# Grouped attention in a decoder kernel: causal zeros written by GpSimd behind the exponential, the second pass without mask matmuls, the last values in the next step

## The chip, the cores and the metric

One core of one Trainium2 chip runs the whole program. The metric is device microseconds of one execution. The engines are PE (TensorE), DVE (VectorE), ACT (ScalarE), GpSimd (POOL in the rows) and SyncE (SP), which only issues DMAs here. The five run in parallel, each in its own order, and wait for one another by semaphores.

## The reference

Two decoder layers of six sublayers on x of [4, 512, 128], float32. The change lies in one sublayer, grouped attention (B = 4, S = 512, 16 heads of 8, 4 groups of 4 heads that share keys and values):

```python
xr = rope(x)
Q = (xr @ Wq).reshape(B, S, N_HEADS, D_K).transpose(0, 2, 1, 3)
Q = Q.reshape(B, N_GROUPS, HPG, S, D_K)
K = (xr @ Wk).reshape(B, S, N_GROUPS, D_K).transpose(0, 2, 1, 3)
V = (xr @ Wv).reshape(B, S, N_GROUPS, D_K).transpose(0, 2, 1, 3)
scores = jnp.einsum('bghsd,bgtd->bghst', Q, K) / jnp.sqrt(jnp.float32(D_K))
mask = jnp.triu(jnp.full((S, S), -1000000000.0, dtype=scores.dtype), k=1)
attn = jax.nn.softmax(scores + mask, axis=-1)
out = jnp.einsum('bghst,bgtd->bghsd', attn, V)
```

The mask is causal: a query sees the keys up to its own place.

## The kernel before

The program runs stage after stage. In `grouped_attention` a first part makes the rotated queries and keys, split into three bf16 parts, and lays them down in DRAM; then the block `ga2` does the attention in 16 steps, `it = GROUPS * b + g`, one for each batch b and group g. Each step works on 512 x 512 scores of four heads, in chunks of 128 (`CH` = 4). It has two passes over the scores:

- First pass, `max_scores(b, g, n)`, n = 0 to 15, c = n // 4 the chunk of queries and i = n % 4 the head: queries on the partitions, keys up to the diagonal on the columns, in `psA[:, n % 2]`. The diagonal block gets the mask by a matmul of `ident_bf` with `mask_bf`, onto which the scores are accumulated. DVE's `maxima` takes the maximum of each row out of it (L1831). Score n waits for maximum n-2, since `psA` has two halves. Below, "score n" and "maximum n" are these.
- The maxima are turned on PE (`turn_maxima`), split into three bf16 parts on DVE (`split_maxima`, five instructions, L1840 to L1844), and sent by SyncE as three further rows of `q` (`put_maxima`, L1660), so that the second pass subtracts them inside the matmul.
- Second pass, `attend(b, g, n)`, n = 0 to 7, c = n // 2 the chunk of keys and n % 2 the pair of heads: keys on the partitions, queries from the diagonal on, two heads, in `psB[:, n % 2]`. ACT takes the exponential of it into `att` (L1810). attend(n) waits for exponential n-2.
- `values(b, g, c)`: four matmuls in float32 (L1754), one a head, accumulate `va` times `att` over c into `psO`; the last increments `o_mm`. ACT copies `psO` (`copy_out`), PE turns the copy (`turn_out`, L1768), and DVE divides by the sums and stores (`output`, L1851 and L1852, two instructions).

The order on each engine is written out by hand in the `step` functions. The first pass runs two steps ahead of the second: the step of `it` has score 2n and 2n+1 of `it + 2` ahead of each attend(n) of `it`, and the turning and the split of `it + 1`. Steps are unrolled for the first and last batch and loop with `Fori` between. SyncE loads `q` and `k` for the next batch when `o_mm` says that the step is done (`q_load`, L1578 and L1580), and behind that the maxima of the next step. GpSimd copies each step's values into `va` and does nothing else. In the first four steps ACT also issues loads of the next stage's weights (`preload`).

Of the kernel before, what the change touches and what calls it, by code (L numbers as in the profile page):

```python
# [20 lines left out]
ALU = mybir.AluOpType  # L21
# [3 lines left out]
P = 128  # L25
BATCH, SEQ, D = 4, 512, 128
TOKENS = BATCH * SEQ
TILES = TOKENS // P
CH = SEQ // P
# [1424 lines left out]
def grouped_attention(nc, A, x, xn, xnT, ident, preload=None):  # L1454
# [12 lines left out]
    with Stage(nc, "ga") as st:  # L1467
# [130 lines left out]
        with Stage(nc, "ga2") as s2:  # L1598
# [18 lines left out]
            m_rows = [s2.sem(f"m_rows{n}") for n in range(2)]  # L1617
            b_scores = s2.sem("b_scores")
            b_exp = s2.sem("b_exp")
            o_mm = s2.sem("o_mm")  # L1620
            o_copied = s2.sem("o_copied")
            o_turned = s2.sem("o_turned")
# [30 lines left out]
            with s2.block() as block:  # L1653
# [26 lines left out]
                @block.gpsimd  # L1680
                def _(pool):
                    pool.memset(va[:, :, :, :], 0.0).then_inc(va_clean, 1)
                    pool.wait_ge(va_clean, 1)
                    pool.memset(va[:, :, :, DH:DH + 1], 1.0).then_inc(va_clean, 1)
                    pool.wait_ge(va_clean, 2)

                    def step(b, g):

                        pool.wait_ge(o_mm, GROUPS * b + g - 1)
                        pool.tensor_copy(va[:, g % 2, :, 0:DH], v[:, bass.ds(CH * b, CH), DH * g:DH * g + DH]).then_inc(va_ready, 1)  # L1690

                    for g in range(GROUPS):
                        if g >= 2:
                            pool.wait_ge(o_mm, g - 1)
                        pool.tensor_copy(va[:, g % 2, :, 0:DH], v[:, 0:CH, DH * g:DH * g + DH]).then_inc(va_ready, 1)
                    with pool.Fori(1, BATCH) as b:
                        for g in range(GROUPS):
                            step(b, g)

                @block.tensor  # L1700
                def _(pe):
# [25 lines left out]
                    def attend(b, g, n):  # L1727

                        it = GROUPS * b + g
                        if n == 0:  # L1730
                            pe.wait_ge(m_rows[g % 2], 96 * b + 48 * (g // 2) + 48)
                        c, pair = n // 2, n % 2
                        if not (first(it, 1) and n < 2):

                            pe.wait_ge(b_exp, 8 * it + n - 1)
                        for i in range(2):
                            keys, queries = k[0:SPLIT + MROWS, g, P * c:P * c + P], q[0:SPLIT + MROWS, g, 2 * pair + i, :]
                            if c < CH - 1:
                                pe.matmul(psB[:, n % 2, i, P * c + P:SEQ], keys, queries[:, P * c + P:SEQ], start=True, stop=True)
                            out = psB[:, n % 2, i, P * c:P * c + P]  # L1740
                            pe.matmul(out, ident_bf[:, :], mask_bf[:, 1, :], start=True, stop=False)
                            mm = pe.matmul(out, keys, queries[:, P * c:P * c + P], start=False, stop=True)  # L1742
                        mm.then_inc(b_scores, 1)

                    def values(b, g, c):

                        it = GROUPS * b + g
                        if c == 0:
                            pe.wait_ge(va_ready, it + 1)
                            if not first(it, 1):  # L1750
                                pe.wait_ge(o_copied, it)
                        pe.wait_ge(b_exp, 8 * it + 2 * c + 2)
                        for i in range(HPG):
                            mm = pe.matmul(psO[VW * i:VW * i + VW, P * c:SEQ], va[:, g % 2, c, :], att[:, g % 2, c, i, P * c:SEQ],  # L1754
                                           start=(c == 0), stop=(c == CH - 1), skip_group_check=True)
                        if c == CH - 1:
                            mm.then_inc(o_mm, 1)
# [13 lines left out]
                    def step(b, g):  # L1771
                        it = GROUPS * b + g
                        for n in range(CH * HPG // 2):
                            if exists(it + 2):
                                for m in (2 * n, 2 * n + 1):
                                    max_scores(*ahead(b, g, 2), m)
                            attend(b, g, n)
                            if n == 1 and exists(it + 1):
                                turn_maxima(*ahead(b, g, 1))
                            if n == 4 and not first(it, 1):  # L1780
                                turn_out(*ahead(b, g, -1))
                            if n % 2 == 1 and n >= 3:
                                values(b, g, (n - 3) // 2)
                        values(b, g, CH - 1)

                    for n in range(CH * HPG):
                        max_scores(0, 0, n)
# [1 line left out]
                    for n in range(CH * HPG):  # L1789
                        max_scores(0, 1, n)  # L1790
                    schedule(pe, step)
                    turn_out(BATCH - 1, GROUPS - 1)

                @block.scalar
                def _(act):
                    def copy_out(it):
                        act.wait_ge(o_mm, it + 1)
                        if not first(it, 1):
                            act.wait_ge(o_turned, it)
                        act.activation(oT[:, :], psO[:, :], ACT.Copy).then_inc(o_copied, 1)  # L1800

                    def step(b, g):
                        it = GROUPS * b + g
                        for n in range(CH * HPG // 2):
                            c, pair = n // 2, n % 2
                            act.wait_ge(b_scores, 8 * it + n + 1)
                            if n == 0 and not first(it, 2):

                                act.wait_ge(o_mm, it - 1)
                            act.activation(att[:, g % 2, c, 2 * pair:2 * pair + 2, P * c:SEQ], psB[:, n % 2, :, P * c:SEQ], ACT.Exp,  # L1810
                                           scale=SCALE).then_inc(b_exp, 1)
                            if n == 1 and not first(it, 1):
                                copy_out(it - 1)
                        if first(it, GROUPS) and preload is not None:
                            preload(act, g, GROUPS)

                    schedule(act, step)
                    copy_out(STEPS - 1)

                @block.vector  # L1820
                def _(dve):
# [35 lines left out]
                    def step(b, g):  # L1857
                        it = GROUPS * b + g
                        for n in range(CH * HPG):
                            if exists(it + 2):  # L1860
                                maxima(*ahead(b, g, 2), n)
                            if n == 5 and exists(it + 1):
                                split_maxima(*ahead(b, g, 1))
                            if n == 9 and not first(it, 1):
                                output(*ahead(b, g, -1))

                    for n in range(CH * HPG):
# [790 lines left out]
```

## Time and profile before

| | us |
|---|---|
| median of 3 runs (1525.8 to 2162.62) | 1527.76 |
| the profiled execution | 1530.27 |
| its span | 1528.5 |
| one steady step of the attention, 393.89 to 404.84 | 10.95 |
| the 16 steps, first exponential to last values, 325.01 to 496.84 | 171.8 |

Busy shares of the span: PE 71%, DVE 62%, ACT 49%, GpSimd 33%. These are averages over stages with different limits; the stage of the change takes some 11% of the span. The span is the profiled execution from its first to its last instruction; its own time is 1.8 us more, and it stands 2.5 us above the median.

### The profile page before, as it was taken

The page shows a single profiled execution, that of the slowest core. Times are in us where ns is not written, and L with a number is a line of the kernel's source. Part 1 is how long each engine was busy: PE and PEld are TensorE (multiplying, and loading weights), DVE is VectorE, ACT ScalarE, POOL GpSimd, SP SyncE. Part 2 cuts the span into 40 slices and gives each one's busy share as a digit, 9 for nine tenths or more (in the row PEclk, how much of TensorE's full clock was granted, in tenths as well). Part 3 has the DMA queues.
Part 4 walks back from the last instruction along what each step waited for, and adds up shares of the span by engine and source line. Part 5 has one row for each costly group of instructions (what it writes and reads, how often), then busy time and mean ns, then how long its engine had stood idle before and what let it go on. Part 6 is the DMA issues. An engine that isn't in the chain of part 4 may idle for free. (4 is left out here: it accounts for less than half of the span.)

```text
span 1528.5 us, 17644 instructions
## 1 busy us (share of the span) xinstructions
PE 1077.8 (71%) x5325; PEld 478.6 (31%) x5326; DVE 945.6 (62%) x1906; ACT 748.7 (49%) x779; POOL 497.3 (33%) x402
## 2 busy tenths in 40 slices
PE   5886932589999549999460658988778877345584
PEld 2533321256665415555230001112112111035353
DVE  6625688367785542222353799999999998265201
ACT  3102622225556302323132159999999999821232
POOL 0000000200000024554110177787886876100463
PEclk9897965669999659999775555555655556565698
DMA  4000000124110101101214100100100000031012
GB/s 157 0 0 25 0 0 17 64 70 164 38 34 12 37 11 28 29 29 28 66 36 142 49 25 21 39 23 24 39 21 28 34 21 1 0 113 32 21 39 75
DMA packets 55665, 60.78 MB, mean 40 GB/s; under 512 B 11130, under 2 KB 43460, under 8 KB 55599
## 3 DMA queue, kind: packets, MB, share of 16 engines
q1 hardware_dynamic: 45294, 45.54, 9.4%
q0 software_dynamic: 3968, 8.13, 2.1%
q10 hardware_dynamic: 6336, 6.29, 1.3%
q8 instruction: 34, 0.56, 0.2%
q14 instruction: 33, 0.26, 0.1%
HBM read 44.35 MB, written 15.34 MB: 39 GB/s over the span
## 5 line engine op out<-in xcount | busy, mean ns | idle before, releaser
L2339 POOL TENSOR_TENSOR hb_t<-hb_t,hb_r 128x1024 f32<-128x1024 f32 x124 | 330.1, 2702 | 199.0 <-ACT hb_r L2285 199.0
L2351 DVE TENSOR_SCALAR hb_dpos<-hb_psR 128x1024 f32<-128x1024 f32 x128 | 155.7, 1217 | 23.4 <-PE hb_psR L2214 18.7
L2223 PE MATMUL hb_psR<-ha_q,ha_k 20*128 20x512 bf16 x256 | 123.0, 578 | 59.8 <-DVE hb_dpos L2351 59.6
L2214 PE MATMUL hb_psR<-ha_q,ha_k 78*128 78x512 bf16 x256 | 123.4, 583 | 48.2 <-DMA ha_k<-hsx 39.7
L2359 DVE SCALAR_TENSOR_TENSOR hb_t<-hb_psR,hb_dpos 128x1024 f32<-128x1024 f32 x128 | 155.1, 1212 | 0.0
L2235 PE MATMUL hb_psO<-hb_t,ha_va 128*9 128x512 f32 x512 | 112.3, 977 | 51.8 <-ACT hb_t L2308 51.8
L1831 DVE TENSOR_REDUCE ga_nm<-ga_psA 128x1 f32<-128x128 f32 (+3 forms) x256 | 112.9, 484 | 47.5 <-PE ga_psA L1717 47.4
L1810 ACT ACTIVATE ga_att<-ga_psB 128x1024 f32<-128x1024 f32 (+3 forms) x128 | 87.0, 709 | 99.9 <-PE ga_psB L1742 99.9
L2368 DVE SCALAR_TENSOR_TENSOR hb_r<-hb_t 128x1024 f32<-128x1024 f32 x64 | 127.3, 1990 | 0.0
L2308 ACT ACTIVATE hb_t<-hb_t 128x4096 f32<-128x4096 f32 x32 | 113.8, 3603 | 0.0
L1315 DVE TENSOR_TENSOR m2x_e_h<-m2x_e_act_out,m2x_e_psG 128x512 f32<-128x512 f32 x39 | 26.8, 688 | 130.6 <-ACT m2x_e_act_out L1284 93.7
L1585 POOL MEMSET ga_q<- 64x8192 bf16 x1 | 6.9, 6920 | 276.4 <-POOLq L1512 276.4
L2285 ACT ACTIVATE hb_r<-hb_r 128x4096 f32<-128x4096 f32 x16 | 57.9, 3619 | 71.1 <-DVE hb_r L2368 70.9
L1284 ACT ACTIVATE m2x_e_act_out<-m2x_e_psU 128x512 f32<-128x512 f32 x39 | 23.3, 598 | 124.8 <-PE m2x_e_psG L1227 124.8
L2214 PEld LDWEIGHTS hb_psR<-ha_q,ha_k 78*128 78x128 bf16 x256 | 19.6, 113 | 168.4 <-DVE hb_t L2359 64.7
L1716 PE MATMUL ga_psA<-ga_mask_bf,ga_ident_bf 128*128 128x128 bf16 x256 | 56.7, 235 | 17.8 <-PEq L250 15.7
L206 PE MATMUL ln_tp<-all_ident,all_xn 128*128 128x128 f32 x80 | 23.9, 455 | 63.0 <-DVE all_xn L165 62.2
L191 ACT ACT_TABLE_LOAD x6 | 7.7, 1283 | 122.5 <-PEq L118 118.5
L2223 PEld LDWEIGHTS hb_psR<-ha_q,ha_k 20*128 20x128 bf16 x256 | 15.8, 103 | 162.6 <-DVE hb_dpos L2351 144.7
L1714 PE MATMUL ga_psA<-ga_k,ga_q 72*128 72x128 bf16 (+2 forms) x192 | 55.1, 298 | 8.4 <-DVE ga_nm L1831 6.3
L2303 ACT ACTIVATE hb_t<-hb_t,ha_one 128x4096 f32<-128x4096 f32 x16 | 59.4, 3711 | 0.2
L2292 ACT ACTIVATE hb_t<-hb_t,ha_one 128x4096 f32<-128x4096 f32 x16 | 59.1, 3694 | 0.0
(448 smaller groups left out, 2289.9 us busy)
## 6 DMA issues: line engine op xcount, KB each, us to landing
ga_q<-qx SPq DMA_DIRECT2D x48, 96.0 KB
ha_q<-hqx SPq DMA_DIRECT2D x48, 96.0 KB
ha_k<-hkx SPq DMA_DIRECT2D x16, 288.0 KB
hsx<-ha_aparts SPq DMA_DIRECT2D x6, 384.0 KB
hy_fwd<-in_const_fwd_dram SPq DMA_DIRECT2D x1, 2048.0 KB, 8.1
hy_inv<-in_const_inv_dram SPq DMA_DIRECT2D x1, 2048.0 KB
f_up<-in_L_ffn_W_dram ACTq DMA_DIRECT2D x4, 512.0 KB, 3.9
f_gate<-in_L_ffn_W_dram ACTq DMA_DIRECT2D x4, 512.0 KB, 5.6
```

The source lines that it names most:

```text
L1810: act.activation(att[:, g % 2, c, 2 * pair:2 * pair + 2, P * c:SEQ], psB[:, n % 2, :, P * c:SEQ], ACT.Exp, scale=SCALE).then_inc(b_exp, 1)
L1831: dve.tensor_reduce(nm[:, g % 2, i, c:c + 1], psA[:, n % 2, 0:P * c + P], AX.X, ALU.max, negate=True).then_inc(a_max, 1)
L2214: mm = pe.matmul(psR[:, dist_slot(n), i, :], k[0:ROWS, it % 2, i0 + i, P * c:P * c + P], q[0:ROWS, it % 2, i0 + i, :], start=True, stop=True)
L2223: mm = pe.matmul(psR[:, side_slot(n), i, :], k[SIDE:SIDE + SROWS, it % 2, i0 + i, P * c:P * c + P], q[SIDE:SIDE + SROWS, it % 2, i0 + i, : ...
L2235: mm = pe.matmul(psO[32 * i:32 * i + VW, :], va[:, CH * (it // G) + c, HPG * (it % G) + i, :], t[:, (2 * it + c % 2) % T_QUADS, 2 * (c // ...
L2292: act.activation(quad(t, it, 1), quad(t, it, 1), ACT.Sqrt, bias=one[:, 0:1]).then_inc(root_ready, 1)
L2303: act.activation(tt, tt, ACT.Ln, scale=2.0, bias=one[:, 0:1]).then_inc(ln_ready, 1)
L2308: act.activation(tt, tt, ACT.Exp, scale=(-1.0, -2.0)[form]).then_inc(w_ready, 1)
L2339: pool.tensor_tensor(tt, tt, r[:, (2 * it + form) % R_QUADS, k, :], ALU.add).then_inc(sum_ready, 1)
L2351: dve.tensor_scalar(dpos[:, n % 2, :], psR[:, dist_slot(n), :, :].rearrange("p i t -> p (i t)"), 0.0, None, ALU.max).then_inc(dpos_ready, 1)
L2359: dve.scalar_tensor_tensor(out=unit(t, n), in0=psR[:, side_slot(n), :, :].rearrange("p i t -> p (i t)"), scalar=CAP, in1=dpos[:, n % 2, :] ...
L2368: dve.scalar_tensor_tensor(out=unit(r, n), in0=tt, scalar=1.0, in1=tt, op0=ALU.add, op1=ALU.mult).then_inc(m_ready, 1)
```

## The change

- GpSimd gets a new function `causal`: behind every second exponential it overwrites the diagonal blocks of chunk c (four heads of 128 x 128) in `att`, in place, with `affine_select`, which keeps what lies on the causal side and puts 0.0 elsewhere. It increments a new semaphore `masked`, for which `values` waits in place of `b_exp`. GpSimd's steps are unrolled for all 16.
- `attend` has no mask matmul: one matmul a head from the diagonal to the end, in place of up to three (16 matmuls of mask fewer in a step, and the diagonal block joined to the rest). The first pass keeps its masks.
- On PE values(0) moves from behind attend(3) to behind attend(4), values(1) from behind attend(5) to behind attend(6), values(2) and values(3) from the end of the step into the next one, behind attend(0) and attend(1). `turn_out` moves from behind attend(4) to behind attend(5).
- On ACT `copy_out` moves from behind exponential 1 to behind exponential 2; on DVE `output` moves from behind maximum 9 to behind maximum 12.

```diff
+                    def causal(b, g):
+                        it = GROUPS * b + g
+                        for c in range(CH):
+                            pool.wait_ge(b_exp, 8 * it + 2 * c + 2)
+                            block_c = att[:, g % 2, c, :, P * c:P * c + P]
+                            pool.affine_select(block_c, block_c, [[0, HPG], [1, P]], ALU.is_ge, 0.0, base=0, channel_multiplier=-1).then_inc(masked, 1)
...
+                    for b in range(BATCH):
                         for g in range(GROUPS):
-                            step(b, g)
+                            if GROUPS * b + g >= 2:
+                                pool.wait_ge(o_mm, GROUPS * b + g - 1)
+                            pool.tensor_copy(va[:, g % 2, :, 0:DH], v[:, CH * b:CH * b + CH, DH * g:DH * g + DH]).then_inc(va_ready, 1)
+                            causal(b, g)
...
-                            if c < CH - 1:
-                                pe.matmul(psB[:, n % 2, i, P * c + P:SEQ], keys, queries[:, P * c + P:SEQ], start=True, stop=True)
-                            out = psB[:, n % 2, i, P * c:P * c + P]
-                            pe.matmul(out, ident_bf[:, :], mask_bf[:, 1, :], start=True, stop=False)
-                            mm = pe.matmul(out, keys, queries[:, P * c:P * c + P], start=False, stop=True)
+                            mm = pe.matmul(psB[:, n % 2, i, P * c:SEQ], keys, queries[:, P * c:SEQ], start=True, stop=True)
...
-                        pe.wait_ge(b_exp, 8 * it + 2 * c + 2)
+                        pe.wait_ge(masked, CH * it + c + 1)
...
-                            if n == 4 and not first(it, 1):
+                            if n < 2 and not first(it, 1):
+                                values(*ahead(b, g, -1), 2 + n)
+                            if n in (4, 6):
+                                values(b, g, (n - 4) // 2)
+                            if n == 5 and not first(it, 1):
                                 turn_out(*ahead(b, g, -1))
-                            if n % 2 == 1 and n >= 3:
-                                values(b, g, (n - 3) // 2)
-                        values(b, g, CH - 1)
...
-                            if n == 1 and not first(it, 1):
+                            if n == 2 and not first(it, 1):
                                 copy_out(it - 1)
...
-                            if n == 9 and not first(it, 1):
+                            if n == 12 and not first(it, 1):
                                 output(*ahead(b, g, -1))
```

On PE, before, from attend(3) (L1739 to L1742) over values(0) to score 8 of a steady step (L1714 to L1717):

```order
L1739 MATMUL ga_psB<-ga_q,ga_k 128x256
L1741 MATMUL ga_psB<-ga_mask_bf,ga_ident_bf 128x128
L1742 MATMUL ga_psB<-ga_q,ga_k 128x128
L1754 MATMUL ga_psO<-ga_att,ga_va 32x512 [waits ga2_b_exp,ga2_o_copied,xa_ln1_stats_ready]
L1754 MATMUL ga_psO<-ga_att,ga_va 32x512 x3
L1714 MATMUL ga_psA<-ga_k,ga_q 128x256 [waits ln1_copied]
```

The same place now, from attend(3) (L1741) over scores 8 and 9 (L1717 to L1720) and attend(4) to values(0) (L1753):

```order
L1741 MATMUL ga_psB<-ga_q,ga_k 128x384
L1717 MATMUL ga_psA<-ga_k,ga_q 128x256 [waits ln1_copied]
L1719 MATMUL ga_psA<-ga_mask_bf,ga_ident_bf 128x128
L1720 MATMUL ga_psA<-ga_k,ga_q 128x128
L1717 MATMUL ga_psA<-ga_k,ga_q 128x256 [waits ln1_copied]
L1719 MATMUL ga_psA<-ga_mask_bf,ga_ident_bf 128x128
L1720 MATMUL ga_psA<-ga_k,ga_q 128x128
L1741 MATMUL ga_psB<-ga_q,ga_k 128x256 [waits ga2_b_exp]
L1741 MATMUL ga_psB<-ga_q,ga_k 128x256
L1753 MATMUL ga_psO<-ga_att,ga_va 32x512 [waits ga2_masked,ga2_o_copied,xa_ln1_stats_ready]
```

Between attend(3) and score 8, which waits for DVE (its semaphore is printed as `ln1_copied`, an old name of the same number), there is no longer a block of values.

On DVE, around the output (L1851, L1852) before:

```order
L1844 TENSOR_TENSOR ga_nmp<-ga_nmr,ga_nmp 16x128
L1831 TENSOR_REDUCE ga_nm<-ga_psA 128x1 x4
L1851 RECIPROCAL ga_rs<-ga_psT 128x16
L1852 TENSOR_TENSOR ga_oa<-ga_psT,ga_rs 128x4x32
L1831 TENSOR_REDUCE ga_nm<-ga_psA 128x1 x12
```

and now (L1853, L1854):

```order
L1846 TENSOR_TENSOR ga_nmp<-ga_nmr,ga_nmp 16x128
L1833 TENSOR_REDUCE ga_nm<-ga_psA 128x1 x7
L1853 RECIPROCAL ga_rs<-ga_psT 128x16
L1854 TENSOR_TENSOR ga_oa<-ga_psT,ga_rs 128x4x32
L1833 TENSOR_REDUCE ga_nm<-ga_psA 128x1 x9
```

Four maxima stood between the split and the output, and seven stand there now: the output is between the first and the second of the four widest.

## Rows read from the trace of the kernel before

**Rows 1.** Windows; columns: stretch, length, busy us of each engine, PEclk, DMA share, GB/s.
```profile
393.89:404.84 10.95, 10.53 (x129) 6.87 (x127) 8.60 (x23) 5.80 (x9) 0.21 (x1) 1.00 0.12 38
481.86:489.71 7.85, 7.11 (x83) 3.97 (x82) 1.82 (x7) 5.69 (x10) 0.00 (x0) 1.00 0.02 4
489.71:497.00 7.29, 6.29 (x74) 3.33 (x72) 0.55 (x2) 5.77 (x10) 0.00 (x0) 1.00 0.00 0
498.00:500.00 2.00, 1.05 (x9) 0.86 (x7) 0.55 (x2) 0.00 (x0) 0.00 (x0) 0.87 0.00 0
```

**Rows 2.** Table of waits, 320 to 500 us: total, times, longest.
```profile
PEld ga_psA L1714 <- DVE ga_nm L1831: 33.4, 69, 0.8
```

**Rows 3.** Timeline of PE in a steady step: start, us, engine, line, operation.
```profile
393.01 0.22 PE L1716 MATMUL ga_psA<-ga_mask_bf,ga_ident_bf 128*128 128x128 bf16 x1
...
393.29 0.22 PE L1741 MATMUL ga_psB<-ga_mask_bf,ga_ident_bf 128*128 128x128 bf16 x1
393.35 0.22 PE L1742 MATMUL ga_psB<-ga_q,ga_k 75*128 75x128 bf16 x1
...
394.60 0.22 PE L1714 MATMUL ga_psA<-ga_k,ga_q 72*128 72x128 bf16 x1
...
396.51 1.06 PE L1754 MATMUL ga_psO<-ga_att,ga_va 128*32 128x512 f32 x8
397.51 0.28 PE L1714 MATMUL ga_psA<-ga_k,ga_q 72*128 72x256 bf16 x1
...
397.76 0.28 PE L1714 MATMUL ga_psA<-ga_k,ga_q 72*128 72x256 bf16 x1
...
399.70 0.85 PE L1754 MATMUL ga_psO<-ga_att,ga_va 128*32 128x384 f32 x8
400.49 0.34 PE L1714 MATMUL ga_psA<-ga_k,ga_q 72*128 72x384 bf16 x1
...
403.97 0.22 PE L1716 MATMUL ga_psA<-ga_mask_bf,ga_ident_bf 128*128 128x128 bf16 x1
```

**Rows 4.** Timeline of PE at the end of the last step but one.
```profile
488.00 1.01 PE L1754 MATMUL ga_psO<-ga_att,ga_va 128*32 128x256 f32 x16
488.94 0.34 PE L1739 MATMUL ga_psB<-ga_q,ga_k 75*128 75x384 bf16 x1
```

**Rows 5.** Timeline of DVE in the same steady step.
```profile
394.97 0.76 DVE L1831 TENSOR_REDUCE ga_nm<-ga_psA 128x1 f32<-128x256 f32 x2 [0.47 <-PE ga_psA L1717]
395.64 0.27 DVE L1840 COPY ga_nmT<-ga_psT 16x128 f32<-16x128 f32 x1
...
396.19 0.28 DVE L1842 TENSOR_TENSOR ga_nmr<-ga_nmT,ga_nmp 16x128 f32<-16x128 f32 x1
...
398.98 0.26 DVE L1851 RECIPROCAL ga_rs<-ga_psT 128x16 f32<-128x16 f32 x1
...
399.59 1.01 DVE L1831 TENSOR_REDUCE ga_nm<-ga_psA 128x1 f32<-128x384 f32 x2
400.98 2.53 DVE L1831 TENSOR_REDUCE ga_nm<-ga_psA 128x1 f32<-128x512 f32 x4 [0.37 <-PE ga_psA L1717]
```

**Rows 6.** GpSimd's groups by line, with mean ns.
```profile
L2339 POOL TENSOR_TENSOR hb_t<-hb_t,hb_r 128x1024 f32<-128x1024 f32 x124 | 330.1, 2702 | 199.0 <-ACT hb_r L2285 199.0
...
L1586 POOL MEMSET ga_k<- 64x2048 bf16 x1 | 1.8, 1798 | 0.0
```

**Rows 7.** Timeline of ACT, the last exponential of the step.
```profile
403.04 0.39 ACT L1810 ACTIVATE ga_att<-ga_psB 128x256 f32<-128x256 f32 x1 [1.17 <-PE ga_psB L1742]
```

**Rows 8.** Line 2368, DVE, a later stage: min/median/max ns.
```profile
L2368 DVE SCALAR_TENSOR_TENSOR hb_r<-hb_t x64: 1206/1916/3441, 854.9 to 1289.2; 128x1024 f32<-128x1024 f32 x64
```

**Rows 9.** Timeline of SyncE's queue in the same step: loads, then maxima.
```profile
393.16 2.64 SPq L1578 DMA_DIRECT2D ga_q<-qx  x3
...
397.06 1.84 SPq L1660 DMA_DIRECT2D ga_q<-ga_nmp  x3
```

**Rows 10.** Line 1660, the maxima's DMAs, 345 to 382 us: issue to landing.
```profile
DMA to landing us min/median/max: 2.2/2.3/5.6
```

More of the change, by code:

```diff
@@ L1619, in grouped_attention @@
             b_exp = s2.sem("b_exp")
+            masked = s2.sem("masked")
             o_mm = s2.sem("o_mm")
@@ L1685, in _ @@
                     pool.wait_ge(va_clean, 2)
[L1687 to L1696, printed above, removed]
+                    def causal(b, g):
[5 more added lines that the diff above has]
+                    for b in range(BATCH):
                         for g in range(GROUPS):
-                            step(b, g)
+                            if GROUPS * b + g >= 2:
+                                pool.wait_ge(o_mm, GROUPS * b + g - 1)
+                            pool.tensor_copy(va[:, g % 2, :, 0:DH], v[:, CH * b:CH * b + CH, DH * g:DH * g + DH]).then_inc(va_ready, 1)
+                            causal(b, g)
                 @block.tensor
@@ L1791, in _ @@
                     schedule(pe, step)
+                    values(BATCH - 1, GROUPS - 1, 2)
+                    values(BATCH - 1, GROUPS - 1, 3)
                     turn_out(BATCH - 1, GROUPS - 1)
```

## Prediction

> **What bounds the kernel now.** First the windows by stage: a step of the grouped attention (one batch, one group; 16 in all) takes 10.95 us at the granted clock 1.00, with PE recorded busy for 10.53 us and DVE for 8.60, ACT for 5.80, GpSimd for 0.21 [rows 1]. That reads like PE alone, but the table of waits says otherwise: PE's weight loads for the first pass's scores waited 33.4 us for DVE's maxima, 69 times [rows 2]. The two engines hold each other: psA has two halves, so score n can't start before maximum n-2 is done. The reader should therefore not ask how busy PE is but which waits close the loop around a step. Followed in the timelines, from score 1 of one step to score 1 of the next, it falls into six stretches [rows 3, 5]:
> (a) PE, score 1 to score 4: 393.01 to 394.60, 1.59 us. (b) Score 4 until DVE takes it: 0.37. (c) DVE, maximum 4 (394.97), maximum 5, the split of the maxima (from 395.64), maxima 6 and 7, which let score 9 start at 397.76: 2.79. (d) PE, score 9 to score 12 (400.49): 2.73. (e) Score 12 until DVE takes it (400.98): 0.49. (f) From there to the next score 1 (403.97): 2.99; DVE runs four maxima of 512 columns in it without a pause (2.53), PE ends it with values(2) and values(3). The sum is 10.96.
> values(0), 396.51 to 397.51 [rows 3], lies inside (c): PE does it while DVE splits. values(2) and values(3) lie inside (f), while DVE does its last maxima.
>
> **The change, part by part.**
> Mask matmuls of the second pass: each occupies 0.06 us of PE (393.29 to 393.35) [rows 3], and joining the diagonal block to the rest costs nothing more, since the columns are the same. Per step 16 go: 0.96 us of PE's issue. That is the gain to be had: 15 us in 16 steps if PE alone set the pace.
> Values: values(0) moves from behind attend(3) to behind attend(4), values(1) from attend(5) to attend(6), values(2) and (3) into the next step behind attend(0) and attend(1). Now the same six stretches:
> (a) loses four mask matmuls (0.24) and takes in values(2) and values(3). Where they are not kept waiting they take 0.94 (488.00 to 488.94) [rows 4]; as two blocks each has a gap of its own ahead of it, which I put at 0.09 (the values' weights are loaded anew, and wait for a semaphore), so 1.12. 1.59 - 0.24 + 1.12 = 2.47, or +0.88.
> (b) stays 0.37.
> (c) stays 2.79: it is DVE's own work. But values(0) is no longer in it, so PE is through with attend(3) at what was 396.3 and stands at score 8 until maximum 6 is done at what was 397.4: about 1.1 us.
> (d) takes values(0), 1.00, in place of values(1), 399.70 to 400.49 or 0.79 [rows 3], and loses 0.24 of masks: 2.70, or -0.03.
> (e) stays 0.49.
> (f) DVE's output moves from behind maximum 9 to behind maximum 12, so its 0.61 us (398.98 to 399.59) [rows 5] falls into the unbroken run: 2.53 + 0.61 + 0.05 for the signal (about what the maximum's end leaves before PE moves) = 3.19, or +0.20. PE's own way through (f) is shorter, since values(2) and (3) are gone from it.
> New loop: 2.47 + 0.37 + 2.79 + 2.70 + 0.49 + 3.19 = 12.01 us, against 10.96: **+1.05 a step**. The masks go where PE waits anyway; the values leave the two places where they were free. Twelve steps have the whole loop: +12.6.
> The ends: step 0 has no values of a step before it and only saves, at most 0.96; I take -0.7. The thirteenth loop lacks the next step's first scores: +0.3. The last two steps have no first pass; ACT and PE share them (5.69 and 7.11 busy of 7.85) [rows 1], the masks save up to 0.96 in the first of them, I take -0.65. Behind the last step values(2) and values(3) must wait for the exponential, then for GpSimd: price of a select plus a signal, +1.0. Together 0.0, so +12.6.
> GpSimd's select: the trace of before has none. Bounds by rate: the memset writes 2048 elements a lane in 1.80 us, so 512 in 0.45; the add with two inputs takes 2.70 mean for 1024, so 1.35 for 512 [rows 6]. A select reads one input and tests an index; I take 1.0, nearer the add, and keep both ends. Four and the copy make 4.2 us of a step of 12: GpSimd is no bound. Does PE wait for it? The last exponential of a step ends at 403.43 [rows 7], 0.5 before the next score 1, or in the new walk about as far; values(3) comes after score 1, attend(0), values(2), scores 2 and 3, attend(1) and the turning of the maxima, some 2.1 later. So a price up to 2.2 is hidden for c = 3, and the others have longer. Hidden by that stretch (a), which it would lengthen one for one beyond 2.2. If code for the select has to be fetched, that is once, ahead of the first exponential, when GpSimd has nothing else to do.
> GpSimd beside DVE: in a later stage one instruction of DVE with both inputs in SBUF takes 1.21 us at least and 3.44 at most, 1.92 at the median [rows 8], with GpSimd adding beside it. The first select starts when the exponential n = 1 ends: attend(1) is through 1.9 after score 1, ACT takes it up 0.2 later and needs about a microsecond, so at some 3.15; the split's first instruction with two SBUF inputs stands at 2.47 + 0.37 + 0.67 + 0.55 = 4.06 (395.64 to 396.19 is the 0.55) [rows 5]. With a select of 1.0 they touch for 0.1, with 1.35 for 0.45, and if the casts between count too, for 0.3 more. This delay is on (c). Between 0 and 0.75 a step; I take 0.2, or +2.4 in twelve.
> On this the page "SBUF — State Buffer" of the Trainium skill (section on the shared pair and its exclusive lock) says that GpSimd and a DVE instruction with two SBUF inputs never share: the later blocks until the earlier has ended. The spread of [rows 8] agrees with that. By it the delay is the whole remainder of the select, which is how the 0.1 to 0.75 above would arise, and never a proportional slowing.
> SyncE: the loads of the next batch wait for o_mm, which now comes some 3 us into the next step; their issue to the first row of maxima takes 3.9 us (393.16 to 397.06) [rows 9]. The maxima are split at 5.5 us in the new step, the queue is free at about 7.0, three issues of 0.61 (the three take 1.84) and the landing (2.3 median [rows 10]) end at 11.2 of the 12.7 at which attend(0) needs them. The slowest landing of the steps with the weights' preload took 5.6 [rows 10]: then up to 1 us is late in three steps. Between 0 and 3; I take 0.
> Sum: 12.6 + 2.4 = +15.0. The profiled execution took 1530.27 us with a span of 1528.5, the median of the runs is 1527.76; against that, **1543 us**.
>
> **Rivals.**
> *The gain arrives.* If PE finds other work in (c) and (f), the 16 masks give up to 0.96 a step, -15, 1513; half of it, with only (a) and (d) shortened by masks, -0.5 a step, 1520. For it: PE is 96% busy (10.53 of 10.95). Against it: that share counts the drain of matmuls, and the order on PE is fixed, so nothing can be pulled ahead into (c). For anything below 1527, 0.10.
> *Selects and DVE collide.* A select of 1.35 and casts that count: 0.75 a step in place of 0.2, +6.6, with the SyncE term +3: 1553. 0.10.
> *GpSimd becomes the bound* (the other side of 2%). Decided by one number, the select's price: from 2.2 us on it lengthens (a), from 2.9 on four of them and the copy are longer than the step. At 4 us, 16.2 a step, +5.2 in 14 steps: 1600. Its rate would have to be three times worse than the add's. 0.05.
> *The clock.* The granted clock stays 1.00 in steps in which PE is busy 6.29 of 7.29 us, and is 0.87 over the two microseconds from 498, of which PE was busy for 1.05: it falls there [rows 1]. The new step has PE busy for some 10.53 - 0.96 = 9.6 of 12.0, 80%, less than the 86% seen with 1.00, but with one hole of no more than 1.1 us. If it fell for part of each step, PE's 9 us of issue double in that part: for a quarter of it, +2 a step, 1572. 0.05.
>
> **Chances and range.** The forecast with its own spread, 1533 to 1552: 0.62; no loss or a small one, 1527 to 1533: 0.08; the gain, below 1527: 0.10; the collision, 1552 to 1558: 0.10; GpSimd or the clock, above: 0.10. The range 1527 to 1557 leaves out 0.20. A measurement of this kernel tells no change of less than about 2% (30 us). Faster by more needs 1497, twice the whole gain of the masks: 0.01. Slower than 1558: 0.09. Between: 0.90.
>
> **What would show it.** A steady step of 11.9 to 12.4 us; a wait of PE of about 1.1 us at score 8, just behind the split; DVE's output between two maxima of 512 columns; values that do not wait for GpSimd; selects of 0.45 to 1.35 us; the clock 1.00 throughout. I am wrong if steps are below 10.9 (DVE's stretches give way), if values wait on the selects, or if the clock in this stage is below 1.00.

## The result, and the profile after it

| | before | after |
|---|---|---|
| median of the runs, us | 1528.55 | 1561.52 (1554.69 to 1565.67) |
| profiled execution, us | 1530.27 | 1554.69 |
| its span, us | 1528.5 | 1552.9 |
| attention, first exponential to last copy of `psO`, us | 171.91 | 190.48 |

The ratio is 1.0197, 95% interval 1.0161 to 1.0232: some 30 us slower, where 15 were forecast. The stage's line is from the windows, cut where each step's first exponential starts (the last one where the last copy starts); the rest of the profiled span differs by 5.8 us.

The windows of the changed kernel, from the first exponential of a step to the next (columns as in [rows 1]), are of two kinds:

```profile
388.42:400.45 12.03, 10.36 (x101) 5.02 (x104) 8.60 (x23) 6.01 (x10) 2.71 (x5) 1.00 0.09 34
400.45:412.41 11.96, 10.29 (x101) 5.02 (x104) 8.60 (x23) 6.01 (x9) 2.71 (x5) 1.00 0.10 34
412.41:426.13 13.72, 11.92 (x101) 5.96 (x104) 8.66 (x23) 6.01 (x9) 2.71 (x5) 0.88 0.08 29
450.07:463.65 13.58, 11.78 (x101) 5.86 (x105) 8.60 (x23) 6.01 (x10) 2.71 (x5) 0.87 0.08 28
```

The first kind is what the walk through the six stretches of the loop in the forecast gave, to 0.05 us (12.01). The second has the same instructions on every engine, and takes 1.6 us more at a lower granted clock; below, this is a fall, and such a step falls. Of the 12 steps from 337.58 to 489.07 five are of the second kind, seven of the first. Against the 12 steps before they are 19.4 us longer (151.49 to 132.10). Twelve steps of 11.96 would be 11.4 longer, by the walk; the other 8.0 are the low clock. The first step and the last two save 0.8. Which part of a step of the second kind it is shows in windows of one microsecond (PE busy, granted clock, DMA share, GB/s):

```profile
453.00:454.00 1.00, 0.65 (x5) 1.00 0.14 25
454.00:455.00 1.00, 0.38 (x4) 1.00 0.12 49
455.00:456.00 1.00, 1.00 (x11) 0.96 0.19 61
456.00:457.00 1.00, 1.00 (x8) 0.50 0.19 75
457.00:458.00 1.00, 1.00 (x11) 0.50 0.25 91
458.00:459.00 1.00, 1.00 (x7) 0.50 0.21 68
459.00:460.00 1.00, 1.00 (x11) 0.84 0.04 12
```

PE has a hole at 453 to 455, and just behind it the granted clock is 0.50 (1.2 in place of 2.4 GHz) until 459. The timeline of PE shows the same in another such step:

```profile
415.50 0.49 PE L1741 MATMUL ga_psB<-ga_q,ga_k 75*128 75x384 bf16 x2
416.96 0.28 PE L1717 MATMUL ga_psA<-ga_k,ga_q 72*128 72x256 bf16 x1 [0.97 <-DVE ga_nm L1833]
...
417.84 1.48 PE L1753 MATMUL ga_psO<-ga_att,ga_va 128*32 128x512 f32 x8
419.25 0.40 PE L1717 MATMUL ga_psA<-ga_k,ga_q 72*128 72x256 bf16 x1
419.44 0.31 PE L1719 MATMUL ga_psA<-ga_mask_bf,ga_ident_bf 128*128 128x128 bf16 x1
```

attend(3), then 0.97 us of waiting at score 8 (line 1717 is before's 1714, 1753 is 1754), a score and attend(4) at full clock, and in the middle of values(0) the clock falls: 1.48 us where [rows 3] has 1.06, a mask matmul 0.31 for 0.22. One step earlier, at a clock of 1.00 throughout, the hole is just as long and nothing falls behind it:

```profile
404.99 0.28 PE L1717 MATMUL ga_psA<-ga_k,ga_q 72*128 72x256 bf16 x1 [0.97 <-DVE ga_nm L1833]
...
405.87 1.07 PE L1753 MATMUL ga_psO<-ga_att,ga_va 128*32 128x512 f32 x8
```

So the hole alone does not decide it. The wait is where the forecast put it. The table of waits, 320 to 520 us, has the sum of all such waits at scores, and what the values wait for GpSimd:

```profile
PEld ga_psA L1717 <- DVE ga_nm L1833: 54.4, 84, 1.4
...
PEld ga_psO L1753 <- POOL ga_att L1694: 8.3, 22, 1.1
```

54.4 us stand against the 33.4 of [rows 2]. DVE's timeline answers to [rows 5], the split and the output in their new places:

```profile
395.75 1.39 DVE L1833 TENSOR_REDUCE ga_nm<-ga_psA 128x1 f32<-128x384 f32 x2
397.05 0.25 DVE L1853 RECIPROCAL ga_rs<-ga_psT 128x16 f32<-128x16 f32 x1
397.44 0.29 DVE L1854 TENSOR_TENSOR ga_oa<-ga_psT,ga_rs 128x128 f32 x1
397.65 2.12 DVE L1833 TENSOR_REDUCE ga_nm<-ga_psA 128x1 f32<-128x512 f32 x4
...
415.17 0.27 DVE L1842 COPY ga_nmT<-ga_psT 16x128 f32<-16x128 f32 x1
...
415.72 0.28 DVE L1844 TENSOR_TENSOR ga_nmr<-ga_nmT,ga_nmp 16x128 f32<-16x128 f32 x1
...
416.50 0.73 DVE L1833 TENSOR_REDUCE ga_nm<-ga_psA 128x1 f32<-128x256 f32 x2
```

The output stands in a run of maxima that has no pause (a row of several names the form of one: x2 is maximum 11 and maximum 12, x4 the other three of 512 columns and the next step's first). The split takes 415.17 to 416.50, 1.33 us, as before (1.32). GpSimd's timeline in the same step has the select ahead of it:

```profile
414.85 0.64 POOL L1694 TENSOR_SCALAR_AFFINE_SELECT ga_att<-ga_att 128x512 f32<-128x512 f32 x1 [2.58 <-ACT ga_att L1812]
```

It ends at 415.49, 0.23 us before the split's first instruction with two inputs in SBUF.

### The profile page after: what moved, and what is told of

It is laid out like the page before. It is cut to its first block and busy times, and to the rows that moved or that the text cites. A ratio compares the mean times of both kernels' runs of the same rounds, so it can differ in the third digit from the quotient of the medians.

```text
span 1552.9 us, 16811 instructions
## 1 busy us (share of the span) xinstructions
PE 1085.6 (70%) x4877; PEld 453.6 (29%) x4878; DVE 953.3 (61%) x1906; ACT 751.4 (48%) x779; POOL 532.8 (34%) x466
## 5 line engine op out<-in xcount | busy, mean ns | idle before, releaser
L2341 POOL TENSOR_TENSOR hb_t<-hb_t,hb_r 128x1024 f32<-128x1024 f32 x124 | 325.8, 2662 | 207.3 <-ACT hb_r L2287 207.3
L2370 DVE SCALAR_TENSOR_TENSOR hb_r<-hb_t 128x1024 f32<-128x1024 f32 x64 | 134.4, 2100 | 0.0
L1315 DVE TENSOR_TENSOR m2x_e_h<-m2x_e_act_out,m2x_e_psG 128x512 f32<-128x512 f32 x39 | 26.8, 688 | 130.6 <-ACT m2x_e_act_out L1284 87.5
L1694 POOL TENSOR_SCALAR_AFFINE_SELECT ga_att<-ga_att 128x512 f32<-128x512 f32 x64 | 40.8, 637 | 168.1 <-ACT ga_att L1812 168.1
L1717 PE MATMUL ga_psA<-ga_k,ga_q 72*128 72x128 bf16 (+2 forms) x192 | 58.2, 309 | 19.7 <-DVE ga_nm L1833 19.4
L1741 PE MATMUL ga_psB<-ga_q,ga_k 75*128 75x512 bf16 (+3 forms) x256 | 58.8, 314 | 1.0 <-ACT ga_att L1812 0.5
```

Of the source, the lines that this page charges most:

```text
L1741: mm = pe.matmul(psB[:, n % 2, i, P * c:SEQ], keys, queries[:, P * c:SEQ], start=True, stop=True)
L2341: pool.tensor_tensor(tt, tt, r[:, (2 * it + form) % R_QUADS, k, :], ALU.add).then_inc(sum_ready, 1)
L2370: dve.scalar_tensor_tensor(out=unit(r, n), in0=tt, scalar=1.0, in1=tt, op0=ALU.add, op1=ALU.mult).then_inc(m_ready, 1)
```

## The experiments

Two theories for what is missing between the 15 us forecast and the 30 measured. **A, the clock**: the walk is as forecast, and what is missing are falls of the granted clock behind holes in PE's work. **B, the selects**: GpSimd's instructions hold up DVE or the values, or the walk is longer than in the sum. Each ratio below is to the kernel before on the same chip, with its 95% interval; windows here are of PE alone: length, PE busy, granted clock, DMA share, GB/s. "Of 12" are the steps behind the first, as above.

**old_places: selects and joined matmuls, everything else where it was.**

```diff
-if n < 2 and not first(it, 1): values(*ahead(b, g, -1), 2 + n)
-if n in (4, 6): values(b, g, (n - 4) // 2)
+if n % 2 == 1 and n >= 3: values(b, g, (n - 3) // 2)
```

values(3) at the step's end, `copy_out`, `turn_out` and `output` are back at before's places too.

> Selects by GpSimd and joined second-pass matmuls as in the changed kernel, but values, copy and output at their places in the kernel before. Theory 1 (the places cost, by the loop between PE and DVE): values(0) fills the split again; a steady step falls from 12.0 us to about 11.4, since values(3) at the step's end waits some 0.7 us for the select of the last chunk; the stage ends 6 us later than in the kernel before and the total is about 1535. Theory 2 (granted clock): the stretches at 0.50 seen in the changed kernel come with the long wait at score 8; here no step shows one. Rival (the selects themselves or the joined matmuls cost): a step stays near 12.0 or above.

Measured: 1558.37 us, ratio 1.016 (1.0107 to 1.0214).

```profile
404.44:416.09 11.65, 10.11 (x100) 1.00 0.10 35
...
428.71:442.97 14.26, 13.18 (x99) 0.72 0.08 27
```

At full clock 11.65 (11.4 was expected), against 10.49 for the same places without selects (joined_only, below): here they cost 1.16 a step, since the values follow their exponential at once, and the weight loads' wait for GpSimd is 20.0 us, against 8.3 at the new places. Eight of the 12 steps have a clock under 0.95, where theory 2 expected none. The fall of one of them begins in values(3), right behind PE's wait for the select (0.65 us for 0.42 at full clock):

```profile
426.51 0.65 PE L1753 MATMUL ga_psO<-ga_att,ga_va 128*32 128x128 f32 x8 [0.61 <-POOL ga_att L1694]
```

So with the selects in, the old places cost more a step than they save, though not all of the values have to move (best_places, below). And falls don't need the new places: they come behind waits for GpSimd too, and behind a hole shorter than 0.97. One step later the same wait of 0.61 has no fall behind it.

**places_only: the kernel before, with the values, copy and output at the new places.**

```diff
-if n % 2 == 1 and n >= 3: values(b, g, (n - 3) // 2)
+if n < 2 and not first(it, 1): values(*ahead(b, g, -1), 2 + n)
+if n in (4, 6): values(b, g, (n - 4) // 2)
```

> The kernel before with its mask matmuls and no selects, but values, copy and output at the places of the changed kernel. Theory 1: a steady step of about 12.5 us (12.0 plus the masks in stretches (a) and (d), 0.24 each), total about 1550 without any fall of the clock. Theory 2: the wait at score 8 is shortened by the masks of attend(3) only, 0.12 of 1.1 us, so if that hole alone makes the clock fall, steps with a stretch at 0.50 appear here as well; if it is the masks' missing work that does, none. Rival (selects or joined matmuls cost): a step near 11.0.

Measured: 1550.62 us, ratio 1.0115 (1.0065 to 1.0165).

```profile
437.65:450.19 12.54, 11.04 (x129) 1.00 0.10 30
```

Every one of the 12 at a clock of 1.00, 12.2 to 12.6 us: the walk with 16 mask matmuls put back, and the ratio is 12 times 1.5 us (18 of 1533). The longer walk is due to the places alone; with the masks in it this trace has no falls. Its hole at score 8 is there, but shorter, since attend(3) still has its two mask matmuls ahead of it:

```profile
417.28 0.28 PE L1714 MATMUL ga_psA<-ga_k,ga_q 72*128 72x256 bf16 x1 [0.84 <-DVE ga_nm L1834]
```

**no_select: the changed kernel without the selects (it leaves out the causal zeros).**

```diff
-pe.wait_ge(masked, CH * it + c + 1)
+pe.wait_ge(b_exp, 8 * it + 2 * c + 2)
-causal(b, g)
```

> The changed kernel without GpSimd's selects: it leaves out the causal zeros of the diagonal blocks, values waits for the exponential. Theory (selects are hidden in a steady step, and DVE's split is not held up by them): steps of 12.0 us as before at the full clock, the stage's end 0.7 us shorter, total within 5 us of the changed kernel. Rival (the selects hold up DVE's split or the values): steps of 11.5 or less.

Measured: 1535.68 us, ratio 1.0104 (1.0058 to 1.0151).

```profile
432.53:446.05 13.52, 11.70 (x101) 0.87 0.09 28
...
459.68:471.64 11.96, 10.29 (x101) 1.00 0.10 32
```

Without the selects the step is still 11.96 at full clock, and 10 of the 12 are at 0.87 or 0.88. So the selects are needed neither for the walk nor for the falls: theory B is out as their cause. It is not settled for the whole time. The ratio lies below both of the changed kernel's (1.0197, and 1.0181 in `after_again`, below), by 12 to 14 us where at most 5 were expected, and its interval ends below that of the first. This trace is of the slowest of its four runs, 5 to 7 us above the other three; whether those fell less often was not recorded, and the changed kernel was not run on this chip. What the selects cost beyond the steps, if anything, stays open.

**double_select: each select issued twice, with a wait between.**

```diff
+pool.affine_select(block_c, block_c, ...).then_inc(again, 1)
+pool.wait_ge(again, CH * it + c + 1)
 pool.affine_select(block_c, block_c, ...).then_inc(masked, 1)
```

> The changed kernel with each block selected twice, the second behind the first, so that the zeros of a block of keys are ready some 0.7 us later (637 ns each in the changed kernel). If the selects are hidden behind the place of the values, as the sum has it, the steps at a granted clock of 1.00 stay at 12.0 us and only GpSimd's busy time doubles, to some 80 us in the selects. If the values stand waiting for GpSimd, each step is 0.5 to 2.5 us longer, up to 14.5, and the values' wait for GpSimd grows from some 8 us to 30 or more.

Measured, in one run: 1563.29 us. All 12 steps are under a clock of 0.95, ten of them 13.5 to 13.9 us at 0.87 or 0.88 (13.3 to 13.7 in the changed kernel), so the 12.0 at full clock that was expected could not be read. The values' wait for GpSimd is 2.2 us in all, not 30. What did show is in DVE's groups by line, 340 to 480 us, here and in the changed kernel's second trace:

```profile
L1847 DVE TENSOR_TENSOR ga_nmr<-ga_nmT,ga_nmp 16x128 f32<-16x128 f32 x10 | 5.7, 570 | 0.3
```

```profile
L1844 DVE TENSOR_TENSOR ga_nmr<-ga_nmT,ga_nmp 16x128 f32<-16x128 f32 x10 | 2.8, 280 | 0.3
```

The timelines of GpSimd and DVE say why:

```profile
382.18 0.64 POOL L1697 TENSOR_SCALAR_AFFINE_SELECT ga_att<-ga_att 128x512 f32<-128x512 f32 x1
```

```profile
382.35 0.60 DVE L1847 TENSOR_TENSOR ga_nmr<-ga_nmT,ga_nmp 16x128 f32<-16x128 f32 x1
382.99 0.21 DVE L1848 CAST ga_nmp<-ga_nmr 16x128 bf16<-16x128 f32 x1
```

DVE's instruction begins inside the select and ends 0.13 us behind it, 0.3 us late in each of ten steps. The page "SBUF — State Buffer" of the Trainium skill (section "Who interferes with whom") says that a DVE instruction with two SBUF inputs contends with a GpSimd instruction that reads SBUF, and that whichever comes second waits until the first is done. The trace agrees, and it is the collision that the forecast priced at 0.2 a step; in the changed kernel the select is over 0.23 us too early for it. The later split also makes the hole at score 8 longer, and every step falls:

```profile
383.91 0.38 PE L1720 MATMUL ga_psA<-ga_k,ga_q 72*128 72x256 bf16 x1 [1.29 <-DVE ga_nm L1836]
```

**values0_back and values0_again: the changed kernel with values(0) behind attend(3) again, ahead of score 8.**

```diff
-if n in (4, 6): values(b, g, (n - 4) // 2)
+if n in (3, 6): values(b, g, (n - 3) // 3)
```

> The changed kernel with values(0) behind attend(3) again, nothing else. Theory 1: the hole at score 8 closes, but values(1) stays away from stretch (d), DVE's run with the output in it becomes the tighter part: a steady step of 11.8 us at the full clock, only 0.2 less. Theory 2 (clock): the hole of 1.1 us is gone, so steps with a stretch at 0.50 vanish, total about 1540. If they remain, the hole at score 8 is not what makes the clock fall.

> The changed kernel with values(0) at attend(3) again, one place ahead of the hole, beside the one filled past the hole. If the place of the widest values behind the hole makes the falls, every step behind the second has a granted clock of 1.00 again and takes 11.7 to 12.1 us, and the median is 8 to 16 us below that of the changed kernel as it stands to the kernel before (a ratio of 1.008 to 1.013). If its first trace happened to have none, some 5 to 9 of the 12 steps are at 0.87 now.

Measured: 1544.15 us, ratio 1.0095 (1.0059 to 1.0131), and 1532.68, ratio 1.0078 (1.0039 to 1.0116). The second trace:

```profile
385.90:397.92 12.02, 10.37 (x101) 1.00 0.10 34
397.92:409.87 11.95, 10.30 (x101) 1.00 0.11 34
```

11.7 to 12.1 at a clock of 1.00 in all 12 (in 11 in the first trace, whose first of the 12 was at 0.58). The walk is the same 12.0, since DVE's split is as long either way; the hole ahead of score 8 is down to 0.21:

```profile
404.08 0.28 PE L1717 MATMUL ga_psA<-ga_k,ga_q 72*128 72x256 bf16 x1 [0.21 <-DVE ga_nm L1833]
```

A ratio of 1.0078 is 12 us (6 to 18 by its interval; the first gives 14.6): the forecast's sum without the collision (12.6), measured. One line of order is worth more than half of the loss.

**fill_hole and fill_again: the changed kernel, with four needless products of 512 columns in the hole.**

```diff
+if n == 4:
+    pe.wait_ge(b_exp, 8 * it + n - 1)
+    for _ in range(4): pe.matmul(psB[:, 0, 0, :], ...)   # ahead of score 8, overwritten by attend(4)
```

> The changed kernel with four needless matmuls of 512 columns ahead of score 8, into a half of psB that attend(4) overwrites: 0.87 us of PE work in the wait of 1.1 us. Results are unchanged. Theory 2 (clock): steps stay at 12.0 us and none shows a stretch at 0.50, the total falls to about 1543. Rival (the falls have another cause, or the clock does not matter for the total): the total stays near 1561, or rises by 16 times some tenths if the fill lengthens the loop.

> The changed kernel with the four needless 512-column products ahead of score 8, beside the unfilled one of the run before on the same chip. If the hole there is what the granted clock falls after, the steps stay at 12.0 us with a clock of 1.00 and this kernel, with more work in it, is some 6 to 16 us faster than the unfilled one. If the hole has nothing to do with it, both have as many low steps and the two medians are within 4 us, or the filled one is slower.

Measured: 1555.6 us, ratio 1.0111 (1.0056 to 1.0166), and 1555.61, ratio 1.0139 (1.0089 to 1.0189), the second beside the unfilled kernel on the same chip:

> The changed kernel once more, beside the filled one of the next run on the same chip. If the falls of the granted clock make the missing time, a second trace has steps of 12.0 us at a clock of 1.00 and steps of 13.6 at 0.87 or less again, the second kind in 4 or more of the 12 steps read, and the median lies some 25 to 35 us above the kernel before. If the first trace was an accident, every step is 12.0 and the median lies 13 to 18 above.

Measured: 1559.85 us, ratio 1.0181 (1.0124 to 1.0237); 9 of its 12 steps at 0.87 or 0.88, and a stage of 196.92 us. Filled, the PE timeline has the products where the hole was, and the window says 12.0:

```profile
408.23 1.04 PE L1776 MATMUL ga_psB<-ga_q,ga_k 75*128 75x512 bf16 x4
...
410.21 1.06 PE L1753 MATMUL ga_psO<-ga_att,ga_va 128*32 128x512 f32 x8
```

```profile
404.79:416.75 11.96, 11.21 (x105) 1.00 0.11 34
```

In both traces every step behind the second of the stage is at 1.00; `fill_hole` had been expected at 1543. The time gains less than the 14 us that 9 falls cost (5 us in the stage, 4 by the medians), because the filled kernel starts the stage lower: its first two steps took 33.4 us at 0.50 and 0.63, against 26.8 in `after_again`. That more work makes a kernel no slower supports A, and the steps themselves bear it out; the medians alone do not (the intervals overlap).

**fill_late: the same four products behind attend(4), so that the hole stays.**

```diff
 attend(b, g, n)
+if n == 4:
+    pe.wait_ge(b_exp, 8 * it + n)
+    for _ in range(4): pe.matmul(psB[:, 1, 0, :], ...)
```

> The changed kernel with the same four needless 512-column products as in the filled one, but behind attend(4), past the hole at score 8, which stays open, and ahead of values(0), the widest run of the values. Four take some 0.86 us at a granted clock of 1.00 and stand on TensorE's part of the step, so a step at 1.00 is 12.0 to 12.9 us. If it is the hole with no work in it that the granted clock falls behind, the falls stay: 5 or more of the 12 steps read have a clock under 0.95, and the time is 5 to 15 us above the filled kernel's. If it is only TensorE's work in the step as a whole that counts, these four help as much as the four in the hole: every step at 1.00.

Measured: 1579.67 us, ratio 1.0371 (1.0329 to 1.0413).

```profile
373.58:390.76 17.18, 16.23 (x109) 0.66 0.34 114
...
420.99:435.45 14.46, 12.79 (x105) 0.88 0.08 28
```

```profile
395.04 0.28 PE L1717 MATMUL ga_psA<-ga_k,ga_q 72*128 72x256 bf16 x1 [0.97 <-DVE ga_nm L1837]
```

None of the 12 is at 1.00, and by the ratios the time is 2.3 to 2.6% above the filled kernel's, 35 to 40 us. Up to 10 of them are the products themselves, which here lie on PE's path (0.86 a step, 12 times); the rest is the clock. PE has the same work in both kernels: what counts is whether the hole is there, not how much is done in a step. That still more work right behind the hole makes the falls worse than in the changed kernel (12 of 12) was not tested by itself.

**output_11: the changed kernel with the output behind maximum 11, out of the run of widest maxima.**

```diff
-if n == 12 and not first(it, 1): output(*ahead(b, g, -1))
+if n == 11 and not first(it, 1): output(*ahead(b, g, -1))
```

> The changed kernel with DVE's output behind maximum 11 instead of 12, nothing else. Theory 1: it leaves the run of four maxima of 512 columns, stretch (f) is 0.2 to 0.6 us shorter, another becomes the tighter: a step of 11.85 us at the full clock. Rival (the output's place costs nothing): 12.0.

Measured, in one run: 1542.03 us on a chip on which the kernel before takes 1518.7. The two full-clock steps take 11.73 and 11.79, where 11.85 was expected; 10 of 12 are at 0.87. The term for the output, +0.20, is right: 12.0 less 11.76.

**joined_only: only the matmuls joined, all at its old place (it leaves out the causal zeros).** The edits of old_places and no_select together.

> Only the second pass without mask matmuls, with everything at the places of the kernel before and no selects: it leaves out the causal zeros. Theory 1 (loop): 10.5 us a step at the full clock in place of 10.95, since half of the masks' time falls where PE waits for DVE anyway. Theory 2 (the removed matmuls are what kept the clock up): stretches at 0.50 appear in many steps and take back 1.6 us or more each, so that the total is not below that of the kernel before although the loop is shorter. Rival (the select's wait in old_places made the clock fall): no such stretches, total about 8 us less than before.

Measured: 1519.12 us (1508.88 to 1526.12), ratio 1.0006 (0.9976 to 1.0036).

```profile
393.05:403.54 10.49, 9.95 (x100) 1.00 0.12 39
```

The step is the 10.5 expected, 0.46 below before's: the most that leaving out the masks can give without moving anything. The trace is of the fastest run, 1508.88; the other nine have granted clocks of 0.699 to 0.714 over the span and come out level with before. In which steps they lost it was not recorded.

**best_places and best2: orders meant to beat both.** In the changed kernel, best_places moves:

```diff
-if n < 2 and not first(it, 1): values(*ahead(b, g, -1), 2 + n)
-if n in (4, 6): values(b, g, (n - 4) // 2)
+if n == 1 and not first(it, 1): values(*ahead(b, g, -1), 3)
+if n == 3: values(b, g, 0)
+if n == 6: values(b, g, 1)
+if n == 7: values(b, g, 2)
-if n == 12 and not first(it, 1): output(*ahead(b, g, -1))
+if n == 11 and not first(it, 1): output(*ahead(b, g, -1))
```

`copy_out` is back behind exponential 1. best2 also turns the maxima behind attend(2) in place of (1), splits them ahead of maximum 8 in place of 6, and turns the output behind attend(4) in place of (5).

> Selects and joined matmuls, with values(0) behind attend(3), values(1) behind attend(6), values(2) behind attend(7), values(3) in the next step behind attend(1), turn_out behind attend(5), output behind maximum 11, copy_out behind exponential 1. Theory 1: each block of values stands where PE would wait; a step of 10.5 us at the full clock, total about 1521 if the clock holds. Theory 2: with 16 matmuls fewer the clock falls in some of the steps, 1.6 us or more each, and the total is between 1521 and 1545.

> The version with values(0) behind attend(3), (1) behind attend(6), (2) behind attend(7), (3) in the next step, and now the maxima turned behind attend(2), split ahead of maximum 8 and the output turned behind attend(4), so that VectorE's split stands behind two more maxima that TensorE needs. The row of TensorE's and VectorE's durations gives 10.26 us a step for it, 10.5 for the version without the last three moves, which took 10.54 to 10.8 in its trace. If the moved split gives what the sum has, steps are 10.3 to 10.6 and the time is 0 to 5 us below that version's, some 0.4 to 0.8 per cent below the kernel before. If the split is late for the next step's first products, steps are 10.8 or more and nothing is won.

Measured: 1516.25 us, ratio 0.9979 (0.9952 to 1.0005), and 1528.5, ratio 0.9973 (0.9937 to 1.0009). Best_places, then best2:

```profile
404.44:415.13 10.69, 10.31 (x102) 1.00 0.12 37
```

```profile
436.73:447.34 10.61, 10.32 (x101) 1.00 0.11 36
```

Most steps take 10.5 to 10.8 in both (10.95 before). Longer are three in best_places (11.11, 11.30, and the first of the 12 with 13.29 at a clock of 0.74) and two in best2 (12.47, and 13.03 at 0.74). The split behind two more maxima wins nothing that shows over best_places. The medians are 0.2 and 0.3% below the kernel before, and both intervals take in no change.

## Why the prediction was wrong

The time lies above the range: 1561.5 against 1527 to 1557. By its own steps:

- **The walk** of six stretches, 12.01 a step: 11.96 and 12.03 measured, and +11.4 us in 12 steps where the sum had 12.6 (one of before's steps took 11.55, not 10.95, and a full-clock step is nearer 11.96 than 12.01). Its parts hold too: 0.97 us at score 8 (about 1.1 forecast), +0.20 for the output (0.24, output_11), and of the 0.96 of masks in a step about half counts, as in the sum, which takes 0.24 out of each of (a) and (d): 0.5 from places_only (12.5) to the change (12.0), 0.46 in joined_only. **Right.**
- **The ends**, 0.0: the first step took 13.22 against 14.00 and the last two with the copy 25.77 against 25.81, both first steps partly at a low clock. Right.
- **The select**, 1.0 us (0.45 to 1.35): 637 ns, the mean of all 64. Its cover held: without any select the step is the same 11.96.
- **The collision**, +2.4: 0 in the changed kernel, since a select of 0.64 is over before the split. The mechanism is real (double_select: 280 to 570 ns); only the select's length was off.
- **SyncE**, 0: no wait for a DMA in the table of waits of these steps.
- **The clock**: this is the step that failed. "What would show it" had the clock at 1.00 throughout, and the rival got 0.05. The prediction set PE's share of the step, 80%, for the rival, and one hole of no more than 1.1 us against it. The share is no witness: the changed kernel's full-clock steps record 86% (10.36 of 12.03), places_only's 88%, and the same order of instructions falls in one step and not in the next. The hole was what mattered, and it was taken for harmless, its clock put at 1.00, without a row that shows one so long at 1.00: the longest wait in [rows 2] is 0.8. The rival had the mechanism, with a size near what came: +2 a step forecast, 1.6 in each step that falls, 5 and 9 of 12 steps in two traces, so 8 and 14 us. The 2.4 us of collision and the 1.2 too many for the walk, neither of which came, hid a part of this: as luck had it, the number missed by less than the clock's share.

The terms as measured: 1530.3 + 11.4 + 1.6 times 5 to 9, less 0.8, gives 1549 to 1555. The profiled executions took 1554.69 and 1556.76; what is left, 2 to 6 us, is put down to the other stages, whose sum lay between 1339 and 1367 us in the traces of this case. The three runs beside the profiled one were 6 to 11 us above it, at granted clocks of 0.700 to 0.709 against 0.716. That they fell more often is a reading of that, and was not seen step by step.

Shown: in the changed kernel's order the hole ahead of score 8 is needed for these falls (values0_again and the two fillings without it, fill_late with it). Its length goes with how often they come: 0.84 us in places_only, none of 12 steps; 0.97 in the changed kernel's two traces, no_select and output_11, 5, 9, 10 and 10 of 12; 1.29 in double_select, all 12. No run makes the hole a little longer or shorter and nothing else, and in old_places falls come behind waits of 0.61, so that this is a row of cases and not a bound. Open: why one step falls and the next, with the same hole, does not; whether the masks in places_only keep the clock up by the shorter hole or otherwise; and what starts the stage at 0.50 in some executions. The last costs some 7 us by itself: the first two steps took 31.3 us in values0_back's trace and 24.5 in values0_again's.

## What to carry to other kernels

A wait that takes the place of free work has two prices: its length on the loop, which a walk through the waits gives to a tenth of a microsecond, and the granted clock behind it. When an edit opens an idle stretch on PE longer than any that the trace of before shows at a clock of 1.00, give a fall of the clock a real chance and a price, and try to move the hole or to fill it. Leave the widest block of matmuls where it covers another engine's private work (here DVE's split); removing matmuls from an engine that waits on a loop gives only what lies on the loop (here half of the masks' 0.96 us a step).

## What the runs showed of the hardware

- A hole of 0.97 us in PE's work, with matmuls on both sides of it, was followed in 5 and 9 of 12 steps by a stretch at 1.2 GHz that began less than 2 us later and made the step 1.6 us longer; in the others nothing followed. The page "TensorE: Matmul & The Clock Gate" of the Trainium skill (section "A second HAM failure mode: psum-queue depth-cycling") says of another kernel that frequent small idle spells between groups of matmuls made the clock swing; the swings between 1.00 and 0.50 in these traces agree with that.
- Needless matmuls in the hole kept the clock at 1.00 in 11 of 12 steps, twice; the same ones behind it in none.
- A select on GpSimd over 128 x 512 float32 takes 637 ns, a quarter of the 2702 of the two-input add of twice as many elements [rows 6]. A two-input DVE instruction that meets it waits until it is over: 570 ns for 280.
